# Expert loop: TensorE keeps expert numbers in registers over iterations and loads them in the fourth block

## The reference

```python
logits = flat @ router_w.T
scores = jnp.sqrt(jax.nn.softplus(logits))
_, idx = jax.lax.top_k(scores + expert_bias, K)          # K = 4, flat: 2048 x 256
topv = jnp.take_along_axis(scores, idx, axis=1)
topv = topv / (topv.sum(axis=-1, keepdims=True) + 1e-20)
...
g = jnp.clip(x @ wg.T, -ALPHA, ALPHA)                    # one expert: 256 -> 128
u = jnp.clip(x @ wu.T, -ALPHA, ALPHA)
return jax.nn.silu(g) * u @ wd.T                         # 128 -> 256
```

## Time and profile before

| | us |
|---|---|
| median of three executions | 641.82 |
| fastest, slowest | 641.24, 646.88 |
| the profiled execution, its own time | 647.46 |
| span of the profiled execution | 645.7 |

### The profile page before, as it was taken

How to read it: one execution, slowest core, us unless ns; L and a number is a source line. 1 busy time by engine, 2 the same in 40 slices (tenths; PEclk the granted TensorE clock), 3 DMA queues, 4 the chain that set the end, 5 groups by cost and what they waited for, 6 DMA issues and landing times.

```text
span 645.7 us, 14200 instructions
## 1 busy us (share of the span) xinstructions
PE 562.6 (87%) x4225; PEld 399.8 (62%) x4226; DVE 433.4 (67%) x1296; ACT 350.5 (54%) x902; POOL 242.9 (38%) x341
## 2 busy tenths in 40 slices
PE   9998798999879699899997987685699999889986
PEld 4654455655469665566766755543477787667864
DVE  5578777886057885677796773444657777667865
ACT  3532666767725667456664545431245665555662
POOL 2523000001332212275535535655424555544530
PEclk9999989999989889999999897877879999999999
DMA  8599716000840007666332151262334454444489
GB/s 245 179 313 299 198 43 158 3 4 3 256 140 1 2 1 226 202 189 204 141 139 95 68 222 68 76 253 91 123 101 144 146 153 145 134 131 143 152 339 369
DMA packets 49552, 95.21 MB, mean 147 GB/s; under 512 B 8596, under 2 KB 40540, under 8 KB 46940
## 3 DMA queue, kind: packets, MB, share of 16 engines
q1 hardware_dynamic: 41820, 75.34, 37.5%
q0 software_dynamic: 7680, 19.21, 8.0%
HBM read 58.54 MB, written 35.59 MB: 146 GB/s over the span
## 4 chain that ended last, share of the span: by engine, by line
PE 51%; DVE 19%; issue 10%; ACT 7%; DMA 6%; POOL 4%; another core or an unknown queue 3%; SPq 0%; ACTq 0%; POOLq 0%; DVEq 0%
PE banks L1464 6%; PE banks L1420 5%; PE banks L1666 5%; PE banks L1279 4%; PE banks L1356 4%; PE banks L1485 4%; DVE mx L1990 3%; DVE mx L1987 3%; PE banks L1677 2%; PE banks L1285 2%; POOL results_by_rank L943 2%; PE banks L1570 2%; DMA results_by_rank<-attn_w,goes 2%; DMA arena<-negT 2%
## 5 line engine op out<-in xcount | busy, mean ns | idle before, releaser
L1123 ACT ACTIVATE arena<-banks 128x512 f32<-128x512 f32 (+1 forms) x256 | 130.2, 551 | 84.9 <-PE banks L1464 47.3
L943 POOL DMA_INDIRECT results_by_rank<-attn_w,goes x80 | 78.0, 975 | 84.3 <-issue 47.5
L1464 PE MATMUL banks<-arena 98*128 98x256 bf16 (+1 forms) x512 | 88.8, 267 | 18.2 <-DMA arena<-negT 4.5
L1987 DVE TENSOR_REDUCE mx<-banks 128x4 f32<-128x1024 f32 x64 | 75.9, 1220 | 19.4 <-PE banks L1420 19.4
L907 POOL DMA_INDIRECT rows_by_expert<-arena,bpb x64 | 63.6, 993 | 59.8 <-ACT arena L1123 24.1
L1420 PE MATMUL banks<-arena 96*128 96x256 bf16 (+1 forms) x512 | 81.4, 263 | 5.1 <-DVE mx L1987 2.5
L1666 PE MATMUL banks<-arena,attn_w 128*128 x320 | 84.5, 387 | 0.4 <-issue 0.3
L1464 PEld LDWEIGHTS banks<-arena 98*128 98x128 bf16 x512 | 43.4, 100 | 52.2 <-ACT arena L1123 14.9
L1990 DVE TENSOR_REDUCE mx<-banks 128x4 f32<-128x1024 f32 (+1 forms) x48 | 57.5, 1222 | 19.6 <-PE banks L1424 17.6
L1420 PEld LDWEIGHTS banks<-arena 96*128 96x128 bf16 x512 | 49.9, 99 | 20.8 <-DVE mx L1987 5.4
L1666 PEld LDWEIGHTS banks<-arena,attn_w 128*128 128x128 f32 x320 | 55.7, 194 | 5.7 <-issue 1.2
(11 more groups left out here) (247 smaller groups left out, 1109.0 us busy)
## 6 DMA issues: line engine op xcount, KB each, us to landing
arena<-parts_dram SPq DMA_DIRECT2D x72, 256.0 KB, 4.2
pvs<-rows_by_expert SPq DMA_DIRECT2D x80, 130.0 KB
parts_dram<-arena SPq DMA_DIRECT2D x24, 384.0 KB, 5.3
arena<-results_by_rank SPq DMA_DIRECT2D x6, 1024.0 KB, 9.8
arena<-in SPq DMA_DIRECT2D x2, 2304.0 KB
rows_by_expert<-zero SPq DMA_DIRECT2D x1, 4160.0 KB, 24.2
arena<-in SPq DMA_DIRECT2D x2, 1920.0 KB
arena<-in SPq DMA_DIRECT2D x3, 768.0 KB
```

What stands on the lines that cost most here:

```text
L943: pool.indirect_dma_start(ys, bass.IndirectOffsetOnAxis(ap=goes[:, j:j + 1], axis=0), yb[j], None).then_inc(y_stored[j], 16)
L1123: act.activation(p_ring[n][:, i % P_RING, :], st_bank[RING_AT[n]["s", b, s] % 3][:, 0:P_WIDTH[n]], ACT.Exp, scale=HD ** -0.5).then_inc(exp ...
L1464: ins = pe.matmul(dst[:, at:at + SEQ - q0], keys, q_rows(n, slice(0, ROWS), s, b, q0, SEQ - q0), start=True, stop=(n == 0 or b < POOL_MASKS))
L1987: ins = dve.tensor_reduce(out, src.rearrange("p (q h k) -> p q h k", q=QT, k=nk), AX.X, ALU.max)
```

## The change

`load_chosen` reads the eight numbers into eight registers that are allocated once. In the loop it is called in the fourth block (`j == 3`), behind that block's gate and up product, with the index `4 * i`; so the fourth block's down product takes its number from the first of the new registers, and the next iteration uses the next ones without loading. The load at the loop's head goes, that in the group behind the loop too, and the one at the exit. Before the loop a second load stands in the eighth block, behind its gate and up product. `block_trips` on TensorE is called before the first block instead of behind the eighth. `finish_step` and `start_step` lose the argument `e`. There are 19 loads in place of 20. Only TensorE's program changes.

```diff
--- before.py
+++ after.py
@@ -1655,10 +1655,14 @@
                     ins = pe.transpose(bank[p][:, k * P:(k + 1) * P], xb[:, q, k * P:(k + 1) * P], ident[:, :])
                 ins.then_inc(xb_turned, 1)
 
-            def experts_of(first):
-                return nc.values_load_multi_w_load_instructions(
-                    eb_i[0:1, bass.ds(first, 8)], engines=[mybir.EngineType.PE], min_val=0, max_val=EXPERTS - 1,
-                    skip_runtime_bounds_check_because="the vector engine clamps every entry to the last expert")[1]
+            chosen_experts = [pe.alloc_register(f"expert{n}") for n in range(8)]
+
+            def load_chosen(first):
+
+                nc.reg_load(chosen_experts, eb_i[0:1, bass.ds(first, 8)])
+
+            def expert(n):
+                return pe.snap(chosen_experts[n], min_val=0, max_val=EXPERTS - 1)
 
             def gate_up(b, e, p):
                 pe.wait_ge(xbT_copied, b + 1)
@@ -1677,43 +1681,46 @@
                 pe.matmul(bank[6 + p][:, 0:D], hidT[:, p, :], experts[:, bass.ds(e * EW + 2 * KD * INNER, D)],
                           start=True, stop=True).then_inc(y_ready, 1)
 
-            def finish_step(s, e, n, p, first=8):
+            def finish_step(s, n, p, first=8):
                 if first >= 3:
-                    down(s - 3, e[n - 3], 1 - p)
+                    down(s - 3, expert(n - 3), 1 - p)
                 if first >= 2:
                     turn_hidden(s - 2, p)
 
-            def start_step(s, i, e, n, q, first=8):
+            def start_step(s, i, n, q, first=8):
                 turn_block(i, q)
                 if first >= 1:
-                    gate_up(s - 1, e[n - 1], 1 - q % 2)
+                    gate_up(s - 1, expert(n - 1), 1 - q % 2)
 
             def four_blocks(i, more):
 
-                e = experts_of(4 * i - 4)
-                finish_step(4 * i, e, 4, 0)
+                finish_step(4 * i, 4, 0)
                 for j in range(1, 4):
-                    start_step(4 * i + j, i, e, 4 + j, j)
-                    finish_step(4 * i + j, e, 4 + j, j % 2)
+                    start_step(4 * i + j, i, 4 + j, j)
+                    if more and j == 3:
+                        load_chosen(4 * i)
+                    finish_step(4 * i + j, j if more and j == 3 else 4 + j, j % 2)
                 if more:
-                    start_step(4 * i + 4, i + 1, e, 8, 0)
-
-            e = experts_of(0)
-            for s in range(8):
-                start_step(s, s // 4, e, s, s % 4, s)
-                finish_step(s, e, s, s % 2, s)
-            start_step(8, 2, e, 8, 0)
+                    start_step(4 * i + 4, i + 1, 4, 0)
+
+            load_chosen(0)
             trips = block_trips(pe)
+            for s in range(7):
+                start_step(s, s // 4, s, s % 4, s)
+                finish_step(s, s, s % 2, s)
+            start_step(7, 1, 7, 3, 7)
+            load_chosen(4)
+            finish_step(7, 3, 1, 7)
+            start_step(8, 2, 4, 0)
             with pe.Fori(2, trips - 1) as i:
                 four_blocks(i, True)
             four_blocks(trips - 1, False)
             end = trips * 4
-            e = experts_of(end - 8)
-            gate_up(end - 1, e[7], 1)
-            finish_step(end, e, 8, 0)
+            gate_up(end - 1, expert(7), 1)
+            finish_step(end, 8, 0)
             turn_hidden(end - 1, 1)
-            down(end - 2, e[6], 0)
-            down(end - 1, e[7], 1)
+            down(end - 2, expert(6), 0)
+            down(end - 1, expert(7), 1)
 
             pe.wait_ge(gu_clipped, end)
             for i, t in enumerate(PE_TILES):
```

## The result

| | before | after |
|---|---|---|
| median | 643.2 us (4 executions, 641.24 to 646.88) | 652.14 us (4 executions, 650.81 to 656.33) |
| the profiled execution, its own time | 647.46 us | 651.77 us |
| its span | 645.7 us | 650.0 us |

The changed kernel is slower by about 9 us where 5 us less were forecast.

A forecast was written before the change was run, and what follows sets the result against it. TensorE was taken to bound the expert loop. Terms of 2.2, 1.4 and 1.2 us sum to 4.8, rounded to 5 us, taken off the 641.82 us median: 636.8 us, range 633.5 to 641.2.

The forecast's parts named there:

- First term: Eight loop iterations up to 541.48 us: from 6.91 to 6.60 us each where quiet, 2.2 us gained in all.
- the branch: TensorE's loop branch, left in place: ScalarE's own branch makes the next down weights late, costing 0.05 us an iteration.
- The load: Register load moved behind the fourth block's gate and up product: 589 ns, mostly covered, costing 0.05 us an iteration.
- Second term: Iterations behind 541 us: 0.2 us each for five quiet ones, 0.1 for four with stalls, 1.4 us gained.
- VectorE's floor: Behind 541 us VectorE's clipping loop needs 6.67 us per four blocks, the new lower limit of an iteration.
- Third term: Loop entry: without both reads there, down weights come at 484.23 instead of 485.46 us, 1.2 us gained.
- The register load by another price: At the skill's 200 ns a register, eight take 1.6 us and the change brings nothing; the sum used the trace.
- The step that failed: Closing the sum: the 5.6 us from profiled execution to median put down to fewer stalls; same 5 us taken off.
- The last lines: Signs of a wrong prediction: longer load, growing row waits, or stalls near 555 and 575 us refilling whatever is won.
- the first rival: More than forecast: 18 iterations give 0.41 us each, with the entry 8.6 us, so 633.2 us; chance 0.2.
- The second: Gain eaten: rows and scatters lose slack in about 50 blocks, 4 to 5 us go back, 640 to 641; 0.2.
- The fourth: Slower: fourth block's rows arrive 2.65 us after issue, delaying the load; 7.0 us an iteration, 642.4 us; chance 0.07.

The follow-up runs named there:

- e14: The whole change, nothing left out, run a third time against the kernel before: 642.82 us against 643.1, ratio 0.9987.
- e15: The change without its early read of the trips (load moved alone), against the kernel before: 640.65 us against 643.1, ratio 0.9897.
- e10: The change without its early read of the trips (load moved alone), against the kernel before: 613.7 us against 616.26, ratio 0.9952.
- b1: The kernel before, nothing changed, profiled once more beside a repeat of the change: 644.52 us.
- e5: The change with the load one block earlier, in the third block, and nine numbers instead of eight: 674.07 us against 644.52 of before, ratio 1.0476.
- a1: The whole change run again, nothing left out, against the kernel before: 651.23 us against 644.52, ratio 1.0096.
- e16: The change plus a 128x128 tensor_tensor on GpSimd behind each loop scatter, against the kernel before: 638.5 us against 643.1, ratio 0.9893.

## Why the prediction was wrong, point by point

**First term, 2.2 us in the eight iterations: about right where no late updates come.** Three executions of before or of its variant with early trips took 57.0 to 57.4 us for them. The change took 55.1 in e14, and with the load moved alone 55.2, 55.8 and 56.9: 2.0 us less in e14, and 0.1 to 2.2 over the whole set; the 56.9 are e15 with its waits. The table's stretch begins one iteration behind the forecast's. From block 5 to 37, the forecast's own, it is 56.0 us in before and 54.0 in e14. A quiet iteration is 6.55 us in e10 and 6.68 in e14, and I had 6.60. Of its two parts, the branch costs the 0.05 us that I gave it: without a load the iteration is still 6.55 us and not 6.50. The load costs 0 in e10's iteration and 0.13 in e14's instead of 0.05. There it starts at 528.1 and takes 817 ns in place of the 589 of the sum, and ends at 528.9; ScalarE's copy had ended at 528.64. The price of the load was taken from rows at the loop's head, where it lies within a scatter; here a scatter starts at 528.39, while it runs. The sequencer's record:

```profile
L1662 PEldq TENSOR_LOAD <-eb_i x1: 817/817/817, 528.1 to 528.1; - x1
```

**Second term, 1.4 us behind block 41: about right in the 618 us comparisons.** There before with early trips took 62.1 and with plain stores 62.4; with the load moved 61.3 and 61.6, and with plain stores 61.0 and 61.1. That is 0.5 to 1.4 us. VectorE's floor came out at 6.75 us an iteration without any load, not 6.67. In the 643 us comparisons stalls of 1 to 4 us lie in this stretch, and it goes from 65.8 and 67.2 to anything between 63.2 and 70.5.

**Third term, 1.2 us at the entry: right for one execution, not for the kernel.** From block 0 to 9 before took 17.0 and 18.9 us and the change 18.1, 17.0 and 16.0. Among the 618 us profiles it is 15.9 to 16.2 where the trips are read late, and 15.4 to 16.7 with the early read. I had taken the entry's stall from one execution, 1.37 us ahead of the down weights at 485.46. In b1 it is 0.70, and in the change the same product still waits 0.75 us at 484.18. That wait is the one that the forecast left there: ScalarE's copy ends at 483.76 + 0.28 = 484.04, and the weights follow by 0.14 us. But in b1 they follow it by 0.14 as well (483.36 and 483.50), with both reads in place. Ahead of it lies a wait for a block's rows that swings more than the term: 0.79 us in before, 1.93 in b1. The rows of b1, then those of the changed kernel in the first comparison:

```profile
480.27 0.20 PEld L1655 LDWEIGHTS banks<-ident,pvs 128*128 128x128 f32 x2 [1.93 <-DMA pvs<-rows_by_expert]
...
483.50 0.30 PEld L1677 LDWEIGHTS banks<-arena,attn_w 128*128 128x128 f32 x2 [0.70 <-issue]
```

```profile
483.76 0.28 ACT L1207 ACTIVATE attn_w<-banks 128x128 f32<-128x128 f32 x1 [0.74 <-issue]
```

```profile
484.18 0.30 PEld L1681 LDWEIGHTS banks<-arena,attn_w 128*128 128x128 f32 x2 [0.75 <-issue]
```

**The register load by another price.** The Trainium skill ("Runtime: NRT & Kernel Launch", instruction fetch and launch sequence) states about 200 ns a register, for loads that it describes as coming from HBM; 1.6 us for eight is an estimate from that. The table here lies in on-chip memory, and all the loads of eight behind a kernel's first took 587 to 917 ns. So the figure doesn't hold for this load; only the nine of e5 come to 2.58 us.

**The step that failed** is the one that closed the sum: "I put the difference down to fewer stalls of the kind at 575.54, which the sum doesn't touch". I took the stalls of the profile as given, and added the gain to them. They are late updates of TensorE, and the change does touch them: in the first comparison and in a1 they fill the first eight iterations too. There the change took 59.8 and 62.0 us against 57.1 and 57.0, so 2.8 and 5.0 us more, where the same code without bursts takes 55.1. The bursts cost 4.8 to 6.9 us in these eight iterations, over twice the term. Nor were the stalls that I called fewer or more a matter of chance. The four blocks around 575.54 (53 to 57) take 7.6 to 11.1 us in all 643 us profiles, 9.3 in before and 9.1 in b1 at the same place, and 6.7 to 7.0 in all twelve of 618 us. The last lines had named this as what would make the prediction wrong, but gave it no price and no place in the range. (The range was also off by its own working: its lower end, 633.5, lies above the first rival's 633.2.)

**The rivals.** The second (rows and scatters lose their slack) had a smaller gain, but not a loss of 9 us, nor the mechanism: in the two profiles with the bursts TensorE has no wait for rows over 0.15 us between 485 and 620 us. The fourth needed rows that come 2.55 us late; the latest landing recorded between 485 and 545 us is 2.25 us after its issue. None of them was the one that came.

**What stays open.** What sets the bursts off isn't settled. Shown is that they come only in 643 us comparisons; that the change ran in three such, had them in its first eight iterations in two profiles and not in the third; that the kernel before had none of the periodic kind in the first eight iterations in two; and that where they are, scatters stand three back to back and pause for 1.9 to 2.4 us. Whether the scatters cause the bursts or pile up behind them could not be told apart, since the kernels made for it met either no bursts at all or a comparison in which the change had none. The traces don't settle it either. In the changed kernel the first of the regular late copies, at 511.57, comes while scatters start 1.34 and 1.66 us apart, and three back to back stand only behind it; in before three stand ahead of the late clip at 573.47. That the quicker loop brings them on is plausible from the first two comparisons, and e14, e15 and e16 speak against it as a rule. A long load isn't needed for it, since a1 has short ones. The early read is not cleared: both profiles with the regular bursts have it, e14 and e16 have it without them, and no kernel with the load moved but without it ran beside a change that had them. So the slowdown was 1.4% in the first comparison and 1.0% in a second, and 0 in a third.

No kernel of this study is surely faster than the change on every chip. The load moved alone lies under before in all three of its comparisons (0.994, 0.995, 0.990) and would be my choice over the change, whose three lie at 1.014, 1.010 and 0.999. The read of the trips, which is all that differs, has shown no gain.

## What to carry to other kernels

Ask of every stall that a sum leaves alone what causes it, and whether the faster loop can have more of it: here they weighed more than all three terms. Price an instruction at the place to which it moves, with its neighbours there (scatters that start while it runs made 593 ns into 767), and not where it stood. And when a change of under 1% is at stake, a comparison on one chip isn't enough; the same change gave 1.014, 1.010 and 0.999 in three comparisons, each with an interval under one per cent wide.

## What the runs showed of the hardware

- The same kernel took 616 to 619 us in three comparisons and 643 to 645 in three others. Nearly all of the 25 us lie ahead of the expert loop: TensorE's first load of expert numbers starts at 439.1 us in e10 and at 464.7 in the changed kernel of the first comparison. Up to 345 us the matmul records cover 313.76 and 312.35 us. Between 345 and 465 us they cover 101.35 and 90.83, at a mean granted clock of 0.93 and 0.86; that stretch is the attention with its own scatters. Whether the lower clock is a cause or follows from the pauses isn't shown; in the loop it is 0.99 (475 to 616.6 us). The rows of this window, first of e10, then of after (length, matmul busy, clock, DMA, GB/s):

```profile
345.00:465.00 120.00, 101.35 (x831) 0.93 0.42 144
```

```profile
345.00:465.00 120.00, 90.83 (x775) 0.86 0.34 124
```

- A load of eight expert numbers into TensorE's registers took 588 to 616 ns in the changed kernel with plain stores (all but the first), and 589 to 866 in its three profiles with scatters. Nine from entry 0 took 1,052 ns, and nine from an entry 4i - 1 took 2,274 to 2,672.
- The traces of the 643 us comparisons hold 7,129 to 7,777 semaphore updates each, those of the 618 us ones 10,132 to 10,250, for programs of about the same length (14,175 to 14,352 recorded instructions). What is missing is not spread evenly. Of the 16 landing updates of each transfer of rows e10 holds 13 to 16 between 485 and 545 us. In a1 most transfers have 4 or fewer, but nine of 31 have all 16, and these stand at the bursts (issued at 522.5, 528.0, 535.2 and 541.0 us). So the record is full at the bursts and has gaps between them. Whether the recording holds the engines up stays open; no run here is without a record.
